# First tiles of the expert stage: one turn moved, one load asked for earlier, eight mark reads left out

## The reference

```
h = layernorm(x) * (1 + ca) + sa                # sa, ca, ... from silu(c) @ wmod
g, a = sigmoid(h Wg + bg), sigmoid(h Wd + bd);  v = h Wv + bv
s[t] = a[t] * s[t-1] + (1 - a[t]) * v[t]        # scan along the sequence
x = x + ga * (s * g)
h = layernorm(x) * (1 + cb) + sb
probs = softmax(h gate_w + gate_b)              # 8 experts, the best 2 are kept
y = sum over the 2 kept: probs[e] * (relu(h w1[e] + b1[e]) w2[e] + b2[e])
out = x + gb * y
```

## Time and profile before

| | |
|---|---|
| median of 3 runs | 450.37 us |
| the profiled execution's own time | 449.75 us |
| its span, first to last instruction | 448.0 us |
| mean granted TensorE clock | 0.903 |
| PE busy, share of the span | 374.5 us, 84% |
| DVE busy | 387.1 us, 86% |
| ACT busy | 320.3 us, 72% |
| POOL busy | 185.7 us, 41% |
| chain that ended last | PE 58%, DVE 24%, issue 8%, ACT 3%, SP's queue 3%, DMA 2% |

### The profile page before, as it was taken

How to read it: one execution, slowest core, us unless ns; L and a number is a source line. 1 busy time by engine, 2 the same in 40 slices (tenths; PEclk the granted TensorE clock), 3 DMA queues, 4 the chain that set the end, 5 groups by cost and what they waited for, 6 DMA issues and landing times.

```text
span 448.0 us, 15323 instructions
## 1 busy us (share of the span) xinstructions
PE 374.5 (84%) x4679; PEld 322.7 (72%) x4680; DVE 387.1 (86%) x1100; ACT 320.3 (72%) x992; POOL 185.7 (41%) x213
## 2 busy tenths in 40 slices
PE   1859889689978982469999999999999999999760
PEld 1424555465555871469999999999999998989660
DVE  4899999998998999648999899999999998888660
ACT  1346998796889450158888888888888888778440
POOL 7023311475678477852333333333333333233321
PEclk9997999988898555569999999999999999999895
DMA  7714551131223244551333323333333332232100
GB/s 225 208 47 129 176 189 56 48 144 71 73 106 126 89 153 152 169 170 44 94 103 92 91 77 93 88 90 95 94 92 89 92 89 73 72 89 72 52 22 9
DMA packets 45943, 45.29 MB, mean 101 GB/s; under 512 B 5934, under 2 KB 40575, under 8 KB 45874
## 3 DMA queue, kind: packets, MB, share of 16 engines
q1 hardware_dynamic: 38208, 27.28, 22.5%
q0 software_dynamic: 6592, 16.92, 10.4%
q10 hardware_dynamic: 1074, 0.23, 0.3%
HBM read 24.52 MB, written 20.81 MB: 101 GB/s over the span
## 4 chain that ended last, share of the span: by engine, by line
PE 58%; DVE 24%; issue 8%; ACT 3%; SPq 3%; DMA 2%; POOL 0%; POOLq 0%; ACTq 0%; DVEq 0%
PE bank L1520 8%; PE bank L1521 8%; PE bank L1522 8%; PE bank L1536 7%; PE bank L1537 7%; PE bank L1538 7%; PE bank L1379 4%; DVE xn L929 3%; PE bank L1533 2%; PE bank L1497 2%; DVE hs L943 2%; DVE st L867 2%; DVE st L873 2%; DVE u L939 2%; DVE pay L952 2%
## 5 line engine op out<-in xcount | busy, mean ns | idle before, releaser
L763 ACT ACTIVATE xs<-bank,b1col 128x128 f32<-128x128 f32 x624 | 165.2, 414 | 30.5 <-PE bank L1522 29.8
L598 POOL DMA_INDIRECT out_dram<-tg,midx x78 | 80.9, 1037 | 160.0 <-DVE tg L1308 144.0
L1520 PE MATMUL bank<-xh,w1hi 128*128 128x128 f16 x624 | 112.2, 225 | 3.5 <-issue 3.1
L1536 PE MATMUL bank<-w2hi,xs 128*128 x624 | 112.7, 219 | 0.0
L1537 PE MATMUL bank<-w2hi,w2f 128*128 x624 | 112.6, 219 | 0.0
L1538 PE MATMUL bank<-w2lo,xs 128*128 x624 | 112.6, 219 | 0.0
L1521 PE MATMUL bank<-xl,w1hi 128*128 128x128 f16 x624 | 112.1, 225 | 0.0
L1522 PE MATMUL bank<-xh,w1lo 128*128 128x128 f16 x624 | 112.0, 225 | 0.0
L1288 DVE TENSOR_TENSOR w2f<-xs 128x1024 f16<-128x1024 f32 x78 | 95.6, 1225 | 2.7
L568 POOL DMA_INDIRECT sorted_rows<-pay,idx x64 | 67.0, 1047 | 30.8 <-issue 18.8
L1286 DVE CAST xs<-xs 128x1024 f16<-128x1024 f32 x78 | 55.1, 706 | 19.2 <-ACT xs L763 15.2
(11 more groups left out here) (233 smaller groups left out, 661.2 us busy)
## 6 DMA issues: line engine op xcount, KB each, us to landing
xs<-sorted_rows SPq DMA_DIRECT2D x78, 130.0 KB
xs<-sorted_rows SPq DMA_DIRECT2D x78, 64.0 KB
sorted_rows<-padt SPq DMA_DIRECT2D x5, 582.0 KB, 5.4
w2f<-in_L_ffn_w_dram SPq DMA_DIRECT2D x4, 512.0 KB, 4.0
xs<-in_L_ffn_w_dram SPq DMA_DIRECT2D x4, 512.0 KB, 3.9
xs<-in_L_attn_x_dram SPq DMA_DIRECT2D x3, 512.0 KB, 8.5
out_dram<-tg,midx POOLq DMA_INDIRECT x78
sorted_rows<-pay,idx POOLq DMA_INDIRECT x64, 2.6
```

Source lines behind the costliest of these rows:

```text
L598: pool.indirect_dma_start(out_rows, bass.IndirectOffsetOnAxis(midx[k][:, t:t + 1], 0), yout[k][:, t, :], None, bounds_check=TOK - 1, oob_i ...
L763: ins = act.activation(hf[e][:, cc, t * P:(t + 1) * P], bank[2 * e + cc // 2][:, o:o + P], ACT.Relu, bias=b1col[:, bass.ds(ex[t][e] * HC + ...
L1520: pe.matmul(o, whi, xh[n % 2][:, rows], start=True, stop=False)
L1536: pe.matmul(o, hh[n % 2][e][:, cc, rows], whi, start=False, stop=False)
```

## The change

PE's turn of tile 1 no longer stands ahead of tile 0's first layer; it stands inside it, between the 24 matmuls of e = 0 and those of e = 1. On SP the first part of tile 2 is asked for right behind the first parts of tiles 0 and 1, ahead of their second parts; the first part of tile 3 comes behind these second parts. `settled` is gone: no mark is made, read or waited for in the first four turns. `landed` is counted once only, when all scatters have landed, and SP waits for that one count at turn 4, as before for two. The number of turns at which this wait stands is now worked out from how many units are sure to be full; the value stays 4 (EARLY_UNITS is 21). SP's wait for the table comes behind its waits for the pads and the early scatters. The table has 3 rows in place of 4.

```diff
-SETTLED_TURNS = 4
+EARLY_UNITS = -(-(FIRST[NSG - 2] * GW - PAIRS * (UNIT - 1)) // UNIT)
+SETTLED_TURNS = EARLY_UNITS // (BUFS * HALVES) - 1
...
-            sp.wait_ge(table_ready, 1)
             sp.wait_ge(pad_out, 16 * len(pad_parts))
             for q in range(RING):
                 sp.wait_ge(scattered[q], 16 * GT * len(range(q, FIRST[NSG - 2], RING)))
+            sp.wait_ge(table_ready, 1)
...
-            def settled(n):
-
-                last = n * HALVES + HALVES - 1
-                sp.wait_ge(landed, sp.value_load(table[2:3, last:last + 1], min_val=1, max_val=2))
-                sp.sem_inc(sp_turn, 1)
-
             for k in range(BUFS):
-                settled(k)
                 load_x(0, k)
+            reload_x(1, 0)
             for k in range(BUFS):
                 load_y(0, k)
-            for it in range(1, PEEL):
+            reload_x(1, 1)
+            for it in range(2, PEEL):
                 if it == SETTLED_TURNS:
                     turns = loop_turns(sp)
-                    sp.wait_ge(landed, 2)
+                    sp.wait_ge(landed, 1)
                 for k in range(BUFS):
-                    if it < SETTLED_TURNS:
-                        settled(it * BUFS + k)
                     reload_x(it, k)
-                    if it > 1:
-                        reload_y(it, k - BUFS)
+                    reload_y(it, k - BUFS)
...
-            pool.sem_inc(landed, 1)
             for g in range(FIRST[NSG - 2], NG):
                 scatter(g)
...
-                mark(dve.tensor_scalar(tcols[:, 2:3], late_place[:, :], 0.0, 1.0, ALU.is_ge, ALU.add))
...
-            def layer1(it, n, ex):
+            def layer1(it, n, ex, between=None):
                 pe.wait_ge(xl_ready, it * BUFS + (n + 1))
                 for e in range(2):
+                    if e and between:
+                        between()
                     after(pe, hf_ready, it * (2 * BUFS) + (2 * n - 1 + e))
...
             for it in range(PEEL):
                 for k in range(BUFS):
-                    turn(it, k + 1)
-                    layer1(it, k, now)
+                    if it * BUFS + k == 0:
+                        layer1(0, 0, now, between=lambda: turn(0, 1))
+                    else:
+                        turn(it, k + 1)
+                        layer1(it, k, now)
```

More of the change, by code:

```diff
@@ L219, in adaln_moe_kernel @@
         pidx = sb("pidx", [P, 1])
-        tcols = sb("tcols", [P, 4])
-        table = sb("table", [4, P], I32)
-        both_codes = sb("both_codes", [4, P // 2], I32)
+        tcols = sb("tcols", [P, 3])
+        table = sb("table", [3, P], I32)
+        both_codes = sb("both_codes", [3, P // 2], I32)
         place = sb("place", [P, 1])
@@ L377, in loop_turns @@
         def loop_turns(eng):
-            return eng.value_load(table[3:4, 0:1], min_val=MIN_TURNS, max_val=MAX_TURNS)
+            return eng.value_load(table[2:3, 0:1], min_val=MIN_TURNS, max_val=MAX_TURNS)
         def last_turn(eng):
-            return eng.value_load(table[3:4, 1:2], min_val=MIN_TURNS - 1, max_val=MAX_TURNS - 1)
+            return eng.value_load(table[2:3, 1:2], min_val=MIN_TURNS - 1, max_val=MAX_TURNS - 1)
         def experts(code):
@@ L477, in _ @@
             load_x(turns, 0)
-            before_last = sp.value_load(table[3:4, 2:3], min_val=MIN_TURNS - 2, max_val=MAX_TURNS - 2)
+            before_last = sp.value_load(table[2:3, 2:3], min_val=MIN_TURNS - 2, max_val=MAX_TURNS - 2)
             for k in range(BUFS):
@@ L1246, in tile_table @@
                 dve.wait_ge(dve_step, done1)
-                mark(dve.tensor_tensor(tcols[:, 3:4], cntt[:, 0:1], pidx[:, :], ALU.subtract))
+                mark(dve.tensor_tensor(tcols[:, 2:3], cntt[:, 0:1], pidx[:, :], ALU.subtract))
                 dve.wait_ge(dve_step, done)
@@ L1270, in _ @@
             dve.wait_ge(tcolsT_ready, 1)
-            dve.tensor_copy(table[:, :], bank[6][0:4, 0:P]).then_inc(table_ready, 1)
+            dve.tensor_copy(table[:, :], bank[6][0:3, 0:P]).then_inc(table_ready, 1)
             dve.wait_ge(table_ready, 1)
-            dve.scalar_tensor_tensor(out=both_codes[:, :], in0=bank[6][0:4, 1:P:2], scalar=float(E * E),
+            dve.scalar_tensor_tensor(out=both_codes[:, :], in0=bank[6][0:3, 1:P:2], scalar=float(E * E),
                                      in1=table[:, 0:P:2], op0=ALU.mult, op1=ALU.add).then_inc(codes_ready, 1)
@@ L1486, in _ @@
             pe.wait_ge(tcols_ready, 1)
-            pe.transpose(bank[6][0:4, 0:P], tcols[:, :], ident[:, :]).then_inc(tcolsT_ready, 1)
+            pe.transpose(bank[6][0:3, 0:P], tcols[:, :], ident[:, :]).then_inc(tcolsT_ready, 1)
             pe.wait_ge(drop_made, 1)
```

## The result

The changed kernel takes 445.08 us, the median of 6 runs (442.52 to 446.23), beside 450.62 us (449.85 to 452.06, 6 runs) for the kernel before: a ratio of 0.987 (95% interval 0.983 to 0.990). The medians differ by 5.5 us here and by 4.8 to 8.0 in the four comparisons, 6.0 on average; 7.3 were forecast. The profiled execution took 442.52 us with a span of 440.7. That it meets the forecast's 442.45 is luck: 1.2 us of its gain came from the first stage, which the forecast put at nothing.

A forecast was written before the change was run, and what follows sets the result against it. PE sets the loop's pace, so only its start counts: 2.8 - 0.46 - 0.57 + 3.54 - 0.65 + 2.64 = 7.3 us, taking the median from 450.37 to 443.1 us; 8-in-10 range 442.0 to 445.6.

The forecast's parts named there:

- Tile 2's late load bounds the start: PE's start: asking for tile 2 earlier removes the 3.54 us that PE idled for it.
- SP's marks: SP behind the table: without `settled` and with the table's wait last, x0b goes out 0.88 us earlier (bounds 0.70 and 1.12).
- The five other marks: SP's remaining `settled` steps ahead of waits for turned tiles: dropping them gains nothing.
- The first matmul 2.8 us earlier: PE, tile 0's first layer: no longer waiting for tile 1, it starts at 183.65 in place of 186.44.
- From the first matmul to the turn of tile 3: PE's stretch from tile 0's first layer at 183.65 to the end of its second layer at 196.2.
- the -0.57: PE, tile 0's first layer: two cold halves take 5.32 us against the old layer's 4.74, a loss of 0.57.
- The turn inside: PE, tile 1's turn between the halves of tile 0's first layer: no wait for its DMA, costs 0.46 us.
- The loop passes it on: Second-stage loop, PE busy 40.00 of 40 us: it passes on unchanged whatever time its start gains or loses.
- VectorE did not bind: Rival at tiles 1 and 2: DVE is the bound, only 1.5 us gained, 448.9 us; chance 0.05.
- The clock did not go back: Rival on PE: short waits keep the clock low, 5.3 us per tile; chance 0.04 for two tiles or more, 0.03 for one.
- Tile 3 didn't bind: Rival on SP's queue: tile 3's second half (x3b) takes 3.5 to 5 us behind second parts; 443.5 to 445 us; chance 0.18.
- Step 7: PE, tile 1's first layer: the clock has risen, so it takes 2.7 us in place of 5.32, gaining 2.64.

The follow-up runs named there:

- the four comparisons: The changed kernel measured four times against the kernel before: medians 445.08, 443.20, 444.49 and 443.34 us, ratios 0.987, 0.984, 0.989 and 0.989.
- the load order alone: Kernel before with tile 2's first part ahead of the second parts, marks still read; run twice: 445.45 and 444.86 us, ratios 0.990 and 0.991.
- the warm kernel: Changed kernel plus 100 matmuls with unread results in PE's idle time; run twice: 440.15 and 439.55 us, ratios to before 0.979 and 0.980.

## Why the prediction was right, and where it was off

1. *Tile 2's late load bounds the start, and its order is the main part.* Right: it gives 4.1 us of stretch with the marks and 3.4 without them, of 6.5 in all, and PE's idle 3.54 us are gone.
2. *SP's marks.* Tile 0 goes out 0.61 us earlier (3.39 to 2.78 after the table), not 0.88; the bound of 0.70 was too narrow. The slow first read did pass to the next read (0.67 against 0.51). The five other marks were put at nothing, and no run tests them alone. What I didn't price is that with the marks tile 3 is asked for so late that it can bind: 17.65 and 17.95 us after the table in the load order alone, 15.32 in the changed kernel (191.57 - 176.25).
3. *The first matmul 2.8 us earlier* is the term that was mis-sized. It begins 6.92 us after the table, against 8.97 before (186.44 - 177.47): 2.05 earlier. Of the 0.74 missing 0.27 are SP's, 0.23 the longer way from issue to turn (2.07 us against 1.84), and 0.22 the start after the low half (183.17 against 182.70: 0.47, just past the upper bound of 0.46, in place of the 0.25 that I took from the middle). These 0.74 are most of what the stretch fell short: 203.56 - 196.2 = 7.36 us were forecast and 6.46 came; the other 0.16 is that 203.56 is where the chain enters the turn, and 203.40 where the turn starts.
4. *From the first matmul to the turn of tile 3* I worked out 196.2 - 183.65 = 12.55 us, and it took 195.72 - 183.17 = 12.55. That is chance: within it two terms offset each other. Tile 0's layer with the turn inside took 5.02 us (183.17 to 188.19) and not 5.75, because the clock rose within it, 4.5 us after its start; so the -0.57 did not come. And PE waited 1.20 us for ScalarE, not 0.65.
5. *The turn inside* was reckoned as a part of the 2.8 gained, and 0.46 lost. Those terms lie on the path, but the prediction didn't ask what the kernel would do without the turn: the same within 0.4 us (19.66 against 19.29 to 19.68), since PE then waits for ScalarE, which begins as soon in either order.
6. *The loop passes it on.* Right: most gaps between outputs are 5.83 to 5.84 us before and after, and from the table to the end all four profiles agree within 1.1 us. The 7.3 us between the two spans are close to 6.46 plus 1.2 of the first stage, less the 0.5 that its last gap lost (10.80 against 10.32).
7. *Rivals.* VectorE did not bind (split of tile 2 6.46 earlier), though it had little to spare: two waits, 0.25 and 0.20 us, between 186.79 and 199.85. The clock did not go back in waits of 0.5 to 0.7 us, and in the warm kernel it stayed at 1.00 through a wait of 1.28 us for ScalarE. The Trainium skill ("TensorE: Matmul & The Clock Gate", A second HAM failure mode: psum-queue depth-cycling) tells of a kernel in which short idle spells between groups of matmuls made the clock go back and forth; no profile here shows that. Tile 3 didn't bind in the changed kernel, but my 2.09 us for its landing were too sure: in two profiles half a first part took 3.84 and 3.39 us from its issue to the turn, with PE waiting for it. The second parts ahead of it, the reason that I gave for this rival, were not what held it. The Trainium skill ("DMA: Bandwidth & Descriptors", Queues, rings and completion order) says that an engine consumes a queue's descriptors in ring order. No profile here shows a cost of that.
8. *Slips in the sums.* Half a warm first layer is 24 x 0.058 = 1.39 us by my own figure; the 1.35 that I used is what it took (189.27 to 190.62). Step 7 gains 5.32 - 2.7 = 2.62, not 2.64. And if x3b takes 3.5 to 5 us from 192.95, it lands 0.25 to 1.75 us after 196.2, not 0.4 to 1.9. None moves the forecast.

## What to carry to other kernels

When one queue issues all loads, put them in the order in which their users stall, not in the order of the tiles: here moving two small loads ahead of four larger ones was worth more than all instructions that were taken out. Price a moved step by what its consumer waits for next; the turn looked like an earlier start and gave nothing, because another engine set the pace. And where runs of one program scatter by more than the effect, measure from an event just ahead of the change: the stretch repeated within 0.4 us while the spans differed by 5.6. A kernel with added instructions may differ for their number alone, in another place, so run one of equal length as a control.

## What the runs showed that was not expected

- The time of PE's stop behind its loop changes with its program's length: 2.6 to 3.4 us of issue, after 6 matmuls, in programs without added instructions, and 1.5 to 2.0, after 32 matmuls, with 200 more. A packet of instructions arrives beside each stop.
- A semaphore count on PE's queue is not free: 56 of them in a row stood in 7.24 us of PE's idle time, so at most about 0.13 us each.
